# A decoder layer on one core: the expert plan, the first gathers and the first expert product moved to earlier places

## What is computed

```python
x = x + gate * h                      # gated linear recurrence over time, on layernorm(x)
x = x + softmax(q k^T) v @ Wo + bo    # cross attention, 16 heads, 77 keys, causal mask, on layernorm(x)
xf = layernorm(x)
scores = xf @ gate_W + gate_b         # 4 experts, each row takes the best 2
h = relu(layernorm(xf @ W1[e] + b1[e]) * g1[e] + be1[e])
y = layernorm(h @ W2[e] + b2[e]) * g2[e] + be2[e]
out = x + xf + sum over the 2 experts of weight * y
```

## Time and profile before

| | |
|---|---|
| median of three runs | 1172.95 us |
| profiled execution, its own time | 1174.56 us |
| its span (first to last instruction) | 1172.8 us |
| PE / DVE / ACT / POOL busy | 94% / 77% / 61% / 38% of the span |
| granted TensorE clock, mean | 0.992 of full |
| turn 7 on PE | some 653 to 703 us |
| expert tiles | some 703 us to the end |

### The profile page before, as it was taken

The page is one execution under the profiler, slowest core; times in us unless marked ns, Lnnn a source line. Parts: engine busy times, 40 slices in busy tenths (PEclk is TensorE's granted clock), DMA queues, the critical chain, the costliest instruction groups (busy, mean ns, idle before and its releaser), DMA issues.

```text
span 1172.8 us, 24294 instructions
## 1 busy us (share of the span) xinstructions
PE 1107.8 (94%) x6017; PEld 906.2 (77%) x6018; DVE 907.9 (77%) x2172; ACT 713.3 (61%) x2080; POOL 443.4 (38%) x394
## 2 busy tenths in 40 slices
PE   6999999999989999999999987989999999999993
PEld 5788888888877787777777765778888888888882
DVE  6888888887874778878878875768777777777774
ACT  4333332333377777768677733767787777777773
POOL 3000000000024333545536452557655555555542
PEclk9999999999999999999999999999999999999997
DMA  8535544455340133143143397885555444444543
GB/s 255 153 135 186 187 144 166 147 179 195 137 146 1 48 98 109 56 125 99 46 144 91 127 259 227 227 216 97 86 84 85 81 80 83 87 80 80 82 66 41
DMA packets 95316, 144.76 MB, mean 123 GB/s; under 512 B 20864, under 2 KB 37428, under 8 KB 94607
## 3 DMA queue, kind: packets, MB, share of 16 engines
q1 hardware_dynamic: 77194, 105.78, 28.6%
q0 software_dynamic: 17216, 35.73, 17.4%
q10 hardware_dynamic: 837, 2.41, 0.6%
HBM read 82.69 MB, written 64.76 MB: 126 GB/s over the span
## 4 chain that ended last, share of the span: by engine, by line
PE 71%; DMA 10%; issue 6%; DVE 5%; ACT 4%; POOL 2%; SPq 1%; POOLq 0%; DVEq 0%; ACTq 0%
PE banks L1119 25%; PE banks L713 20%; PE banks L778 7%; PE banks L925 5%; DMA out<-rows,scatter_rows 5%; PE banks L890 3%; PE banks L903 3%; DMA rows<-slot_table 2%; ACT rows L1328 2%; PE banks L1131 2%; PE banks L1147 2%; PE banks L751 1%; PE banks L914 1%; PE banks L839 1%; DVE rows L1898 1%
## 5 line engine op out<-in xcount | busy, mean ns | idle before, releaser
L1119 PE MATMUL banks<-operands 128*128 x1608 | 388.9, 397 | 18.1 <-DVE operands L1596 7.1
L1119 PEld LDWEIGHTS banks<-operands 128*128 128x128 f32 x1608 | 297.9, 189 | 82.1 <-issue 13.8
L713 PE MATMUL banks<-operands 128*128 128x512 f32 (+2 forms) x1224 | 292.8, 396 | 3.5 <-DVE operands L1596 3.5
L713 PEld LDWEIGHTS banks<-operands 128*128 128x128 f32 (+1 forms) x1224 | 227.8, 194 | 49.1 <-DVE operands L1596 3.7
L1596 DVE TENSOR_TENSOR operands<-banks,operands 128x512 fp32r<-128x512 f32 (+1 forms) x232 | 157.1, 685 | 28.9 <-ACT operands L1211 25.3
L1211 ACT ACTIVATE operands<-banks 128x512 fp32r<-128x512 f32 (+1 forms) x232 | 136.3, 597 | 66.2 <-PE banks L804 33.0
L1328 ACT ACTIVATE rows<-banks,score_shift 128x77 f32<-128x77 f32 x512 | 158.5, 337 | 13.3 <-DVE score_shift L1820 13.0
L1211 ACT ACTIVATE operands<-rows 128x512 fp32r<-128x512 f32 (+2 forms) x77 | 54.0, 710 | 163.6 <-DVE rows L1667 139.2
L2655 POOL DMA_INDIRECT out<-rows,scatter_rows x67 | 106.4, 1588 | 107.5 <-DVE rows L2391 64.6
L1521 ACT ACTIVATE banks<-banks,param_cols 128x128 f32<-128x128 f32 x268 | 99.2, 430 | 78.0 <-PE banks L1147 77.9
L2564 POOL TENSOR_TENSOR rows<-rows,score_rec 128x1232 f32<-128x1232 f32 x32 | 72.8, 2276 | 139.3 <-DVE score_rec L1828 139.3
(11 more groups left out here) (187 smaller groups left out, 1639.4 us busy)
## 6 DMA issues: line engine op xcount, KB each, us to landing
expert_parts<-operands SPq DMA_DIRECT2D x32, 512.0 KB, 3.0
operands<-expert_parts SPq DMA_DIRECT2D x8, 2048.0 KB, 12.0
rows<-in_x SPq DMA_DIRECT2D x8, 1024.0 KB, 5.4
rows<-in_L_ffn_W SPq DMA_DIRECT2D x32, 256.0 KB, 3.5
x_rows<-rows SPq DMA_DIRECT2D x8, 1024.0 KB, 4.3
rows<-x_rows SPq DMA_DIRECT2D x8, 1024.0 KB, 5.8
xf_rows<-rows SPq DMA_DIRECT2D x32, 256.0 KB, 2.4
out<-rows SPq DMA_DIRECT2D x32, 256.0 KB
```

Of the source, the lines that this page charges most:

```text
L713: last = nc.tensor.matmul(dst, stationary(a, k), moving(b, k), start=(t == 0 and k == 0), stop=(t == len(terms) - 1 and k == n_k - 1))
L1119: last = nc.tensor.matmul(dst, stationary[:, a, k, :], weights[:, w, bass.ds(e, 1), a2, k, :].rearrange("p e f -> p (e f)"), start=False, ...
```

## The change

DVE: parts 1 and 2 of `plan_early` move from the last turn to turn 6, part 1 behind `out_lo(6, 2)`, part 2 to the end of the turn; `gather_rows(0, 0)` and `(0, 1)` move forward to where part 2 stood. POOL: the two gathers of tiles 0 and 1 move from behind to in front of `normalise(7, 2)`. PE: `prime` of tile 0's bank moves in front of `rows_in(0, 0)`; `first_product(0, 0)` moves from behind the tail projections and positions to in front of `gate_scores(7)`. ACT: `fill_first(0, 0)` moves into the last turn, in front of `out_hi(7, 3)`, with its waits; the expert number is loaded ahead of `rows_hi(0, 0)`. No work is added or removed.

```diff
--- before.py
+++ after.py
@@ -1070,15 +1070,17 @@
 
                 probs_to_keys(c, 3, 0)
                 pe.wait_ge(s_read, TPC * HPG * KC * NCH)
+                pe.wait_ge(experts_ready, 1)
+                prime(m1_bank[0])
                 rows_in(0, 0)
                 probs_to_keys(c, 3, 1)
                 xf_to_features(c - 1, c, 2)
                 attend(c, 3)
 
                 xf_to_features(c - 1, c, 3)
-                pe.wait_ge(experts_ready, 1)
-                prime(m1_bank[0])
                 rows_in(0, 1)
+                pe.wait_ge(plan_ready, 1)
+                first_product(0, 0, expert_at(pe, 0))
                 gate_scores(c)
 
             pe.wait_ge(consts_done, 1)
@@ -1191,8 +1193,6 @@
             for j in range(TPC):
                 project(last, tail, j)
             positions(last - 1, tail, "r")
-            pe.wait_ge(plan_ready, 1)
-            first_product(0, 0, expert_at(pe, 0))
             for j in range(2):
                 xf_to_features(last, tail, j)
             pe.wait_ge(mm_read, mm_num(tail, "o3") + 1)
@@ -1472,8 +1472,13 @@
                 base_in_place(c - 1, 1)
                 out_hi(c, 2)
                 pT_even(c, 3, 0)
+                act.wait_ge(plan_ready, 1)
+                first_expert = expert_at(act, 0)
                 rows_hi(0, 0)
                 pT_even(c, 3, 1)
+                act.wait_ge(b1_in, 16)
+                act.wait_ge(primed, 1)
+                fill_first(0, 0, first_expert)
                 out_hi(c, 3)
 
             act.wait_ge(g_done, KC * NCH)
@@ -1570,10 +1575,6 @@
 
             last_turn(NCH - 1)
             route_weights(NCH - 2)
-            act.wait_ge(b1_in, 16)
-            act.wait_ge(plan_ready, 1)
-            act.wait_ge(primed, 1)
-            fill_first(0, 0, expert_at(act, 0))
             for j in range(2, TPC):
                 base_in_place(NCH - 2, j)
             for j in range(2):
@@ -2188,6 +2189,8 @@
                 if back2:
                     slots(c - 2, c, parts=(0,))
                 out_lo(c, 2)
+                if planned:
+                    plan_early(1)
                 if back:
                     turn_xf(c - 1, 0)
                     turn_xf(c - 1, 1)
@@ -2209,6 +2212,8 @@
                 out_lo(c, 3)
                 if back:
                     choose(c - 1, c, (1,))
+                if planned:
+                    plan_early(2)
 
             def first_turn():
                 max_scores(0, 1, 1)
@@ -2250,7 +2255,6 @@
             def last_turn(c):
                 pT_odd(c, 0, 0)
                 max_scores(c, 1, 1)
-                plan_early(1)
                 x2_rows(c - 1, c, 0)
                 pT_odd(c, 0, 1)
                 count(c - 2)
@@ -2259,7 +2263,8 @@
                 max_scores(c, 2, 0)
                 ln3_pair(c - 1, 0)
                 read_positions(c)
-                plan_early(2)
+                for i in range(2):
+                    gather_rows(0, i)
 
                 max_scores(c, 2, 1)
                 out_lo(c, 0)
@@ -2274,8 +2279,6 @@
                 out_lo(c, 1)
 
                 max_scores(c, 3, 1)
-                for i in range(2):
-                    gather_rows(0, i)
                 pT_odd(c, 2, 0)
                 invert_sums(c, 3)
                 pT_odd(c, 2, 1)
@@ -2609,12 +2612,12 @@
                 ln3_pow(c - 1, 0)
                 scatter(c - 3, 0)
                 scatter(c - 3, 1)
+                for u in range(2):
+                    gather(0, u)
                 normalise(c, 2)
                 for i in range(2):
                     pool.wait_ge(base_out[i], 16 * 2 * (c - 1))
                 widen_gate(wide_gate, gate_w)
-                for u in range(2):
-                    gather(0, u)
                 normalise(c, 3)
                 ln3_pow(c - 1, 1)
                 scatter(c - 3, 2)
```

## The result

Measured in the same rounds, the changed kernel has a median of 1176.18 us (18 runs, 1172.47 to 1179.14) against 1172.68 us before (18 runs): ratio 1.0035, 95% interval 1.0023 to 1.0047, that is 2.7 to 5.5 us slower. The profiled execution took 1174.45 us with a span of 1172.7 us. The spans of the two profiled executions are thus alike (1172.8 and 1172.7), although the kernels are not: the stages ahead of the change ran 2.6 us quicker in the second. So a place must be read against a mark that stands ahead of all edits. I take the start of `attend(6, 2)` on PE (643.52 us in the trace before, 640.92 after) and call times from it **marks**.

What follows compares the result with a forecast made beforehand. PE, busy 94% of the span, was taken to bound the kernel. 2.09 - 0.5 + 1.6 - 0.1 - 1.01 + 0.32 = +2.4 us on the median 1172.95 gave 1175.4; range 1171.8 to 1178.7.

Steps and rivals of the forecast that it cites:

- Rival (a): PE's clock falls in the longer gap: 1177.0 us, + 4.0; chance 0.18.
- Plan part 1, +2.09, no cover: Turn 6: eight DVE steps in front of a copy PE already waits for delay PE by 2.09 us.
- Plan part 2 free, 0.5 us recovered, +1.6 at `attend(7, 0)`: End of turn 6: some 0.9 us of DVE steps cost PE nothing; PE wins back 0.5, leaving +1.6.
- The gathers hold the third normalise, +1.6: POOL, turn 7: gathers in front delay the normalise PE waits for by 1.6 us more, bounds 0 to 2.6.
- The gather's wait goes, +2.4 at `attend(7, 3)`: At `rows_in(0, 0)`: PE's wait of 1.01 us goes, priming costs 0.32, leaving `attend(7, 3)` 2.4 late.
- Slots land in time: First slot loads land by about 664 us, DVE asks at 666.3 in `gather_rows`: no wait, cover 2.3 us.
- Rival (b): Slots land late and DVE stands at `gather_rows(0, i)`: +4.0 if 2 us later, 1177.0 us; chance 0.08.
- The product's move is neutral: `first_product(0, 0)` in front of the gate products costs nothing, with 1.9 us of cover; its 0.9 gain is worth nothing.
- The chain of 35.6 us: SyncE's transfers from `load_expert(1)`, after `attend(7, 3)`, to tile 0's second product take 35.6 us and shift by 2.4.
- Rival (c): SyncE's chain shrinks in a drier queue, PE's own path decides: +0.6, 1173.6 us; chance 0.13.
- one of the signs that the prediction had named for being wrong: Tile 0's second product released by PE's or DVE's own work instead of by SyncE's queue.

Runs made afterwards that it cites:

- e3: Kernel before with only the plan's parts 1 and 2 moved to turn 6, part 1 behind `out_lo(6, 2)`; ratio to before 1.0007.
- e7: Kernel before with only both plan parts moved, to the end of turn 6 behind `choose`; ratio to before 0.9977.
- e10: The changed kernel once more, unaltered, for a second profile; ratio to before 1.0035.
- e2: Changed kernel with `first_product(0, 0)`, `prime` and `fill_first` back at their old places, plan and gathers still early; ratio to before 1.0019.
- e6: Changed kernel with SyncE's second group of slot loads right behind the first; ratio to before 0.9977.
- e4: Kernel before with only the product moved (`prime`, `fill_first`, `first_product(0, 0)`), plan and gathers at old places; ratio to before 0.9996.
- e1: Changed kernel with POOL's two gathers back behind the third normalise; ratio to before 1.0008.
- e5: Kernel before with only SyncE's second group of slot loads moved right behind the first; ratio to before 0.9998.
- e8: Kernel before with the product's move of e4 and the slot loads ahead of e5; ratio to before 0.9982.
- e9: Kernel before with both plan parts at the end of turn 6 and the second slot loads ahead; ratio to before 0.9990.
- e11: As e9, with the gathers' row numbers early and the product in front of the gate products; ratio to before 0.9985.
- e12: The kernel of e7 built again and measured in new rounds; ratio to before 0.9985.

## Why the prediction was right

The time, 1175.4 forecast and 1176.18 measured, lies in the range, and the direction was right; the size was not: + 2.4 us forecast, 2.7 to 5.5 measured. Rival (a), 1177.0 or + 4.0, lies in that interval, and its mechanism, a fall of the clock in the longer gap, is what the trace shows. The range took the time in because it reached up to (a), to which the prediction gave a chance of 0.18 only. By the points of the prediction:

1. **Plan part 1, +2.09, no cover: shown.** e3 has 2.12, and e7, with the same steps behind `choose`, has 0.00 at the same place.
2. **Plan part 2 free, 0.5 us recovered, +1.6 at `attend(7, 0)`: shown as a sum.** e3 and e10 have 1.46 for both parts together.
3. **The gathers hold the third normalise, +1.6: shown.** 1.8 in e2, e6 and e10. The lower bound of the range, 0, was too kind; the scatter, gather, normalise sequence has no gap.
4. **The gather's wait goes, +2.4 at `attend(7, 3)`: mis-sized.** The wait did go, but the lag was 4.9 us, and 4.0 in e10. The term that was missing is the clock. The 4.88 us fall into 1.46 for the plan (e3), 0.84 for the clock behind the plan's gap (22.06, e3 21.22), 1.81 for the gathers, 1.49 for the clock behind theirs, and 0.72 back from the gather's wait and the priming. The clock makes 2.3 of it. The second of these falls is rival (a); the gap of 2.34 us at the end of turn 6 was not thought of as one in which the clock could fall.
5. **Slots land in time: right.** The first loads go out at 658.11 and no DVE wait for a DMA stands at `gather_rows(0, i)`. Rival (b) didn't happen.
6. **The product's move is neutral: supported.** e4 has a ratio of 0.9996. Pairs that differ in the product agree within their intervals: e1 and e3 (1.0008, 1.0007; e1 also has the row numbers early), e5 and e8, e9 and e11.
7. **The chain of 35.6 us is fixed and only shifts: wrong.** From `load_expert(1)` to g2 it was 35.1 us before, 33.8 in the changed kernel, 30.4 to 36.9 over all. Rival (c) had this mechanism, at a size of 1.8; 1.3 of it came. And at 720.14 PE waits for SyncE no longer, one of the signs that the prediction had named for being wrong: the first product of tile 2, slowed by a third fall of the clock, runs into the second product of tile 0 without a gap (7.34 us for the two). That hangs on the fall. In e10, the same kernel without it, SyncE releases this product again, 34.9 us behind `load_expert(1)`:

```profile
720.99 3.01 PE L1121 MATMUL banks<-operands 128*128 x12 [1.48 <-issue]
725.93 2.98 PE L1121 MATMUL banks<-operands 128*128 x12 [1.93 <-SPq L627]
```

Points 4 and 7 have opposite signs, 2.5 us more and 1.3 less, and only together do they come out near the forecast. That is luck.

The share of the clock is shown for these profiles, not for the kernel's runs as a whole. The profile before, with a mean clock of 0.992, is one of few falls: the kernel before has means of 0.987 to 0.990 over its runs in the four rounds of experiments. On one chip the 12 runs of e10 have 0.9865 and the 29 of the kernel before 0.9871, which is 0.7 us of the span and no more than its own uncertainty. So how much of the 2.7 to 5.5 us is the clock stays open.

The late plan was no bottleneck. What it released, two slot loads and a gather, was worth 1.0 us of PE's time, and was paid for with 1.5 for the plan and 1.8 for the gathers, on the two engines that PE waits for most closely, and with the falls of the clock. No kernel of these beats the one before by more than a quarter of a per cent; the lowest ratios are 0.9977 (e6, e7; e7 again, as e12, has 0.9985) and 0.9982 (e8).

## What to carry to other kernels

Before small steps are moved earlier on an engine, look for the next instruction behind their new place whose result the busiest engine already waits for: eight steps of a quarter of a microsecond cost their full 2.1 us in front of such a copy. Behind it they cost nothing at that place, but 1.1 us at the next copy, so look one copy further too. An indirect DMA costs the queue that issues it 1.0 to 1.3 us here, even if its data is wanted much later, so it goes behind, not in front of, the operation that others wait for. And a wait on a transfer in a queue full of megabytes isn't removed by taking one small load out of the way: see which large transfer takes its place in the order.

## What the runs showed of the hardware

**The clock falls behind gaps of 1.5 to 3 us, but not each time.** With the same code up to there, the gap of 2.35 us at the end of turn 6 was followed by half clock in three profiles (the changed kernel, e1, e2) and not in three others (e3, e6, e10). Behind the gap at the third normalise it fell in the changed kernel (2.89 us of gap), in e6 (2.90) and in e10 (2.03), and not in e2 (2.10). It fell behind shorter gaps too. The first product of tile 1, in e6 and in e7:

```profile
710.44 4.54 PE L1120 MATMUL banks<-operands 128*128 x12 [1.50 <-ACT banks L1513]
```

```profile
706.69 3.01 PE L1119 MATMUL banks<-operands 128*128 x12 [1.50 <-ACT banks L1509]
```

In dense work such a fall takes 1.5 to 1.6 us (4.54 and 4.58 for 3.0). At `attend(7, 0)` and `attend(7, 2)` 0.8 and 1.1 to 1.5 us of it arrived. The Trainium skill, "TensorE: Matmul & The Clock Gate", section "HAM oscillation — how this bites in real kernels", tells of such falls behind waits for a DMA; these profiles agree, and show them behind waits for VectorE, ScalarE and GpSimd too.

**Indirect DMAs beside VectorE.** The gathers took 1.00 and 0.98 us at their new place, and a scatter at 687.29 beside `ln3_apply` 1.60, as one did before (1.64). The Trainium skill, "SBUF — State Buffer", section "Who interferes with whom", says that GpSimd stands still while VectorE holds the ports that they share; the trace agrees in both.

**A DVE copy came late without a wait that the kernel asks for.** `pT_odd(7, 1, 1)` waits only for PE's transposes, which had ended 1.6 to 1.9 us before it started in e3 and e4 (e4 is the same as before in this stretch). "remote" means that the profile names no engine of this core:

```profile
676.14 0.69 DVE L1838 COPY whole_operands<-banks 77x512 f32<-77x512 f32 x1 [2.71 <-remote]
```

```profile
674.48 0.69 DVE L1839 COPY whole_operands<-banks 77x512 f32<-77x512 f32 x1 [2.59 <-remote]
```

PE lost 1.5 and 1.9 us to it, and in e4 and e9 the clock fell behind it as well. The marks of `attend(7, 1)` against `attend(7, 0)` show it, at 0.8 to 2.0 us, in e1, e2, e3, e4, e9, e10 and e11, and not in before, the changed kernel, e5, e6, e7, e8 and e12. What it is no run settles; it is as large as any of the edits, and a reason not to compare two single profiles by their spans.
